# Late queries for heads 8 to 15 in the cross-attention, and the context columns of the first latent batch placed behind the small experts

## The chip, the cores and the metric

The kernel runs on 1 core of one Trainium2 chip, as one program. The metric is the device time of one execution in microseconds (us): 3016.62 us is the median of 3 runs of the kernel before (3016.44 to 3020.77).

A core has five engines that run side by side and meet only at semaphores: TensorE (PE, matmuls; its weight loads are shown as PEld), VectorE (DVE), ScalarE (ACT), GpSimd (POOL) and SyncE (SP, which here only issues transfers). Matmul results land in PSUM, where this kernel holds eight banks: `psG` (four), `psT` (two, for transposes) and `psO` (two, for attention outputs).

## The reference, cut to what matters

Sixteen batches of 112 tokens of width 256 go through four residual blocks. `T` is 112, `D` is 256, `H` is 16 heads of 64, and the context of a batch has `S` = 375 rows.

```
# block 1: self-attention, cross-attention over the context, gated MLP
h1 = adaln(x, t, ...);  x = mha(h1, h1, ...) + x
h2 = adaln(x, t, ...);  x = mha(h2, context, attn2_wq, attn2_wk, attn2_wv, ...) + x
h3 = adaln(x, t, ...);  x = glu_ff(h3, ...) + x

# block 2: 64 small experts (256 -> 128 -> 256), top 8 of them per token, and a shared expert
routed = einsum(expert_act * router_mask, expert_down);  x = x + shared + routed

# block 3: latent attention; keys and values come from the context and the latents together
x = layer_norm(ctx) * ln1_w + ln1_b
lat = layer_norm(layernorm(x_tokens)) * (ln2...) * (1 + scale) + shift
q = lat @ Wq.T;  kv = concat(x, lat) @ Wkv.T            # 375 + 112 = 487 rows
out = softmax(q k / 8) v @ Wo.T

# block 4: 8 large experts, one per token
```

All of it is in f32. The experts' outputs of block 2 are needed by a token before its latent row can be normalised, but the 375 context rows of block 3 depend on the inputs alone.

## The kernel before, in words

**Order of work.** Each engine has its own hand-written instruction stream, in the order of the Python code. A wait is `wait_ge(semaphore, value)`. The class `Tally` counts events, so that both sides of a semaphore know the number they want. Nothing is scheduled by a planner: the order written is the order run.

**Banks for projections.** `bank_for_act` and `bank_for_dve` hand out `psG` banks 0 and 1 to results that ScalarE evacuates, and 2 and 3 to results that VectorE evacuates. Before a bank is reused, PE waits until the evacuation two jobs back is done. `evacuated()` waits for all of them. `held(a, d)` waits for all but the last `a` and `d`, and says which banks the attention must still wait for.

**Block 1** is `batch(b, begin, last)` on each engine, b = 0 to 15. In its cross-attention half PE projects the values of the context (`values2`), transposes the normalised rows `hn2` (`transpose_h`), transposes those of the next batch (`hn1`), projects the queries for heads 0 to 7 (evacuated by ScalarE) and heads 8 to 15 (evacuated by VectorE), runs two small matmuls for the router of the batch before (`tile_ranks`, which wait for a mask that VectorE makes in `choose`), and enters `attention`. There a step `s` of the loop issues the scores of the two heads of pair `s`, the transposes of the probabilities of pair `s-1`, and the value products of pair `s-2`. VectorE takes each head's maximum (`nmax`), ScalarE the exponentials (`probs`); half of the transposes are copied by VectorE, the other half by ScalarE. In the gaps VectorE runs `slots(b-1, i)`, small steps of the router.

**Between block 1 and 2** the last tile is normalised by GpSimd (`normalise_tile`), routed, and its slots are scattered to a table in DRAM (`scatter_tile`). From that the block tables come (`tables0`), then the shared expert (`shared`), in whose loop VectorE also measures the context rows of the first latent batch (`measure_context(0)`), and then GpSimd normalises them (`context_rows(0)`) before it starts the gathers for the experts.

**Block 2** is `blocks0`: 176 blocks of 128 gathered rows. The gathered rows `xg`, their transposes `xT` and the outputs `ysb` lie in the tile that later holds the keys (`flat` is a view of `kT2`). ScalarE stores each output block to `expert_rows` in DRAM.

**Block 3** starts when the stores have landed: GpSimd fetches eight rows for each token (`fetch0`), VectorE adds them up with their weights (`add_rows`, eight instructions) and takes mean and variance (`measure_latents`), GpSimd normalises twice (`latents`, which signals `lat_ready`), PE transposes context and latents together (`transpose_kv`), the copies to `ctxT` apply weight and bias (`copy_kv`), and then come keys (`keysL`, eight products of 487 columns), values (`valuesL`, four chunks of keys, in two halves each) and queries (`queriesL`). `transpose_kv(1)` for the second batch stands before the first attention. From there a steady loop, `batchL`, has each attention followed by the keys and values of the next batch, while VectorE adds the rows of the batch after that.

## Time and profile before

| what | value |
|---|---|
| median of 3 runs | 3016.62 us |
| the profiled execution | 3016.74 us, its span 3015.0 us |
| PE busy | 2805.8 us (93%) |
| DVE busy | 1519.9 us (50%) |
| ACT busy | 1047.2 us (35%) |
| POOL busy | 905.7 us (30%) |
| granted TensorE clock, mean | 0.975 of full speed |
| block 1 | from the start to about 1372 us |
| tables and shared expert | about 1372 to 1437 us |
| block 2, small experts | about 1437 to 1739 us |
| block 3, latent attention | about 1739 to 2798 us |
| tables and block 4, large experts | about 2798 us to the end |

The span is what the profiler saw, from the first to the last instruction of the core. The execution's own time is 1.7 us longer. PE is the engine to look at: where it is busy without gaps at full clock, only fewer matmuls help, and where it stands still, the row behind the gap says who released it. A releaser called "issue" is one that the profile doesn't show. In a timeline row the columns are start, duration, engine, line, operation, output<-input, shapes, count of merged instructions, and in brackets the idle time just before and who ended it. Every f32 matmul appears as two records, so that a projection of 8 matmuls reads x16 (times two chunks of the inner dimension, x16 for four output tiles).

### The profile page before, as it was taken

Reading aid. Unit: us, or ns where it says so; the run is one execution under the profiler, and the core shown is the slowest. Engines: PE = TensorE matmul, PEld = TensorE weight load, DVE = VectorE, ACT = ScalarE, POOL = GpSimd, SP = SyncE. Lnnn points to the kernel's source line nnn. Section 1 sums busy time; section 2 is a strip of 40 time slices with the busy share of each in tenths; the row PEclk is TensorE's granted clock in tenths of the full one; section 3 lists DMA queues with packets and bytes.
Section 4 is the critical chain, followed back from the end, with each engine's and each line's share of the span. In section 5 each row is a group of like instructions: output and inputs, shape, how many; then the busy total and the mean of one; then the engine's idle time right before and its main releaser. Section 6 shows DMA issues by size and latency. Waiting matters only on the chain.

```text
span 3015.0 us, 58447 instructions
## 1 busy us (share of the span) xinstructions
PE 2805.8 (93%) x17275; PEld 1929.8 (64%) x17276; DVE 1519.9 (50%) x4444; ACT 1047.2 (35%) x2721; POOL 905.7 (30%) x1782
## 2 busy tenths in 40 slices
PE   7999999999999999986999948999999999999795
PEld 5777767667777777664788725555555656565574
DVE  4455555555455555555555524555555555554332
ACT  1433333433334333331343313443334433343121
POOL 1021222211221112213555435443443434420212
PEclk9999999999999999997999979999999999999898
DMA  6000000000000000003788831000010000100432
GB/s 218 8 6 7 7 7 7 7 7 7 7 2 7 5 7 7 7 3 118 222 257 266 144 113 33 23 19 19 19 36 20 19 19 26 30 2 3 151 131 61
DMA packets 89264, 154.75 MB, mean 51 GB/s; under 512 B 16964, under 2 KB 64720, under 8 KB 87664
## 3 DMA queue, kind: packets, MB, share of 16 engines
q1 hardware_dynamic: 39760, 85.60, 8.6%
q0 software_dynamic: 21072, 42.53, 6.1%
q10 hardware_dynamic: 28368, 25.83, 2.5%
q8 instruction: 32, 0.52, 0.1%
q14 instruction: 32, 0.26, 0.0%
HBM read 121.93 MB, written 31.98 MB: 51 GB/s over the span
## 4 chain that ended last, share of the span: by engine, by line
PE 85%; DVE 5%; issue 5%; DMA 2%; POOL 1%; ACT 1%; DVEq 0%; POOLq 0%; ACTq 0%
PE psG L895 13%; PE psG L889 13%; PE psG L883 12%; PE psG L905 8%; PE psT L856 7%; PE psO L869 7%; PE psG L841 6%; PE psG L1221 5%; PE psG L1298 2%; PE psO L1313 2%; PE psO L1233 2%; PE psG L1212 1%; DVE nmax L1792 1%; PE psG L805 1%; PE psT L796 1%
## 5 line engine op out<-in xcount | busy, mean ns | idle before, releaser
L895 PE MATMUL psG<-W,ctxT 128*125 128x512 f32 (+2 forms) x896 | 406.7, 597 | 0.0
L1441 ACT ACTIVATE probs<-psG,nmax 112x375 f32<-112x375 f32 (+1 forms) x512 | 317.2, 621 | 237.8 <-DVE nmax L1792 237.8
L889 PE MATMUL psG<-ctxT,W 128*128 128x375 f32 (+1 forms) x1024 | 392.7, 531 | 1.1 <-ACT ctxT L1628 1.1
L1792 DVE TENSOR_REDUCE nmax<-psG 112x1 f32<-112x375 f32 (+1 forms) x512 | 285.2, 601 | 128.6 <-PE psG L841 128.3
L856 PEld LDWEIGHTS psT<-ident,probs 112*125 112x125 f32 (+2 forms) x1792 | 203.2, 166 | 190.6 <-ACT probs L1441 146.8
L883 PE MATMUL psG<-hT,W 128*128 128x112 f32 x2560 | 308.8, 280 | 3.2 <-ACT hT L1466 3.2
L883 PEld LDWEIGHTS psG<-hT,W 128*128 128x128 f32 x2560 | 297.1, 195 | 17.5 <-ACT hT L1466 10.5
L889 PEld LDWEIGHTS psG<-ctxT,W 128*128 128x128 f32 x1024 | 190.1, 190 | 166.5 <-issue 115.1
L856 PE MATMUL psT<-ident,probs 112*125 112x112 f32 (+2 forms) x1792 | 255.6, 278 | 31.9 <-ACT probs L1441 23.6
L895 PEld LDWEIGHTS psG<-W,ctxT 128*125 128x125 f32 (+2 forms) x896 | 159.2, 186 | 173.0 <-issue 171.2
L841 PE MATMUL psG<-kT,qT 64*112 64x375 f32 (+1 forms) x1024 | 249.9, 565 | 11.3 <-ACT ctxT L1628 10.7
L869 PE MATMUL psO<-probsT,v 125*64 125x112 f32 (+2 forms) x3584 | 228.5, 266 | 0.0
L635 POOL DMA_INDIRECT kT<-normed_rows,ids x176 | 166.4, 945 | 138.1 <-PE psG L1212 135.5
L869 PEld LDWEIGHTS psO<-probsT,v 125*64 125x64 f32 (+2 forms) x3584 | 173.5, 136 | 28.6
L1221 PE MATMUL psG<-W,kT 128*128 x704 | 185.9, 386 | 0.2 <-issue 0.2
L905 PE MATMUL psG<-W,oT 128*112 128x256 f32 x768 | 174.7, 381 | 4.0 <-DVE oT L1756 3.9
L1796 DVE COPY probsT<-psT 125x336 f32<-125x336 f32 (+1 forms) x256 | 142.6, 557 | 52.0 <-PE psT L856 52.0
L905 PEld LDWEIGHTS psG<-W,oT 128*112 128x112 f32 x768 | 133.3, 177 | 40.8 <-issue 14.7
L267 POOL TENSOR_SCALAR ve<-mv 112x1 f32<-112x1 f32 x64 | 12.3, 192 | 461.8 <-DVE mv L1844 387.2
L1449 ACT ACTIVATE probsT<-psT 125x336 f32<-125x336 f32 (+1 forms) x256 | 125.4, 490 | 44.0 <-PE psT L856 43.1
L582 POOL DMA_INDIRECT slot_table<-stt,st x128 | 122.4, 957 | 53.1 <-issue 40.2
L659 POOL DMA_INDIRECT mlp<-expert_rows,st x128 | 121.2, 946 | 47.2 <-issue 34.1
(348 smaller groups left out, 4109.5 us busy)
## 6 DMA issues: line engine op xcount, KB each, us to landing
expert_rows<-kT ACTq DMA_DIRECT2D x197, 128.0 KB, 1.8
W<-in_ew SPq DMA_DIRECT2D x64, 384.0 KB, 4.6
W<-in_ew SPq DMA_DIRECT2D x8, 2048.0 KB, 8.8
ctxT<-in_ctxT SPq DMA_DIRECT2D x16, 375.0 KB, 3.1
kT<-in_ctx SPq DMA_DIRECT2D x16, 375.0 KB
W<-in_eb SPq DMA_DIRECT2D x8, 640.0 KB, 10.1
normed_rows<-hrow SPq DMA_DIRECT2D x32, 112.0 KB, 1.9
kT<-normed_rows,ids POOLq DMA_INDIRECT x197, 4.1
```

Of the source, the lines that this page charges most:

```text
L635: nc.gpsimd.indirect_dma_start(out=xg[:, j % 4, :], out_offset=None, in_=hd, in_offset=bass.IndirectOffsetOnAxis(ap=ids[:, j:j + 1], axis= ...
L841: nc.tensor.matmul(psG[0:T, bank, 0:keys], qT[DH * i:DH * i + DH, s, :], kT[DH * i:DH * i + DH, s, 0:keys], start=True, stop=True).then_in ...
L856: mm = nc.tensor.transpose(psT[0:kn, i, c * T:(c + 1) * T], probs[:, 2 * (u % 2) + i, k0:k0 + kn], ident[0:T, 0:T])
L869: mm = nc.tensor.matmul(psO[DH * i:DH * i + DH, u // 4, (u % 4) * T:(u % 4 + 1) * T], v[0:kn, c, h * DH:(h + 1) * DH], probsT[0:kn, u % 2, ...
L883: mm = nc.tensor.matmul(bank[:, j * T:(j + 1) * T], wt[:, c, n0 + j * P:n0 + (j + 1) * P], hT[:, c, :], start=(c == 0), stop=(c == DC - 1))
L889: mm = nc.tensor.matmul(bank[:, 0:n], wt[:, c, n0 + j * P:n0 + (j + 1) * P], src[:, c, 0:n], start=(c == 0), stop=(c == DC - 1))
L895: mm = nc.tensor.matmul(bank[0:kn, 0:512], src[:, c, k0:k0 + kn], wt[:, c, n0 + half * 512:n0 + (half + 1) * 512], start=(c == 0), stop=(c ...
L905: mm = nc.tensor.matmul(bank[0:T, 0:D], oT_[:, c, :], wo[:, c, :], start=(c == 0), stop=(c == n - 1))
L1221: mm = nc.tensor.matmul(psG[:, 2 + j.m2, 0:256], xT[:, j.m2, c, :], weights(c, rank), start=(c == 0), stop=(c == DC - 1))
L1441: nc.scalar.activation(probs[:, 2 * (s % 2) + i, 0:keys], psG[0:T, score_banks(s)[i], 0:keys], ACT.Exp, bias=nmax[:, h:h + 1], accum_out=r ...
L1792: nc.vector.tensor_reduce(nmax[:, 2 * s + i:2 * s + i + 1], psG[0:T, score_banks(s)[i], 0:keys], AXX, ALU.max, negate=True).then_inc(max_r ...
L1796: nc.vector.tensor_copy(probsT[0:size, (s - 1) % 2, 0, 0:nb * T], psT[0:size, 0, 0:nb * T]).then_inc(copied_dve, 1)
```

## The change

It has two parts.

**Late queries (block 1).** The projection for heads 0 to 7 moves ahead of the transposes of `hn1`. The projection for heads 8 to 15 leaves its place ahead of the attention and is issued inside it, in step 1, behind the scores of pair 1 and ahead of the first transposes of probabilities. It goes to bank `psO[:, 1]`, which the attention's value products don't touch before pair 4. VectorE's copy of it moves from ahead of the attention to behind the maxima of pair 1. PE waits for that copy at pair 4.

**Context columns first (block 3).** The transfer of the context rows moves from behind the projection weights to the end of block 1, ahead of the shared expert's weights. VectorE measures them at once, and GpSimd normalises them between `normalise_tile(15)` and `scatter_tile(15)`. The buffers of the experts (`xg0`, `xT0`, `ysb0`) move out of the keys' tile into the weight tile `W`. Behind the experts PE transposes the context alone, makes the keys of its 375 columns and the values of the first three chunks, and only then takes the latents: their transposes, the queries, the latents' 112 key columns (a product of their own) and the last chunk of values. The normalisation of latent batch 0 moves from GpSimd to VectorE (`latents0`). `transpose_kv(1)` moves behind the first attention.

```
 # PE, block 1
+            def late_queries():
+                dve.next()
+                project_T(wq2, hT2, 512, 4, psO[:, 1, :]).then_inc(dve_full, 1)
+                return dve.now()
...
                 values2(2, sides=(1,))
+                pe.wait_ge(w_in["q2"], 16)
+                pe.wait_ge(act_evac, hT2_done)
+                project_T(wq2, hT2, 0, 4, bank_for_act()).then_inc(act_full, 1)
+                q2_done = act.now()
                 if not last:
                     pe.wait_ge(hn1_ready, b + 2)
                     transpose_h(hn1)
-                pe.wait_ge(w_in["q2"], 16)
-                pe.wait_ge(act_evac, hT2_done)
-                project_T(wq2, hT2, 0, 4, bank_for_act()).then_inc(act_full, 1)
-                project_T(wq2, hT2, 512, 4, bank_for_dve()).then_inc(dve_full, 1)
                 if not begin:
                     tile_ranks(b - 1)
-                banks = held(0, 1)
+                pe.wait_ge(act_evac, q2_done)
+                banks = held(1, 1) if not last else held(0, 1)
 # PE, attention: step s of the loop
+                    if s == PAIRS // 2 and late:
+                        pe.wait_ge(dve_evac, queries_done)
...
+                    if s == 1 and late:
+                        queries_done = late()
 # DVE, attention
+                    if s == 1 and late:
+                        late()
                     if s:
                         dve.wait_ge(probsT_ready, u0 + 2 * s - 1)
...
-                copy4(qT2[:, 4:8, :], QSCALE)
 # SP
             sp.wait_ge(dve_evac, BLOCK1_JOBS)
+            sp.dma_start(ctxr[:], a["ctx"][0].rearrange("(c p) d -> p c d", p=SC)).then_inc(ctxr_in, 16)
             sp.dma_start(shw, a["shw"]).then_inc(sh_in, 16)
...
-            sp.dma_start(ctxr[:], a["ctx"][0].rearrange("(c p) d -> p c d", p=SC)).then_inc(ctxr_in, 16)
 # POOL
             normalise_tile(B - 1)
+            context_rows(0, S0.normed)
             scatter_tile(B - 1)
...
-            context_rows(0)
             experts(L0E, S0)
...
-                latents(b)
+                if not isinstance(b, int) or b:
+                    latents(b)
                 fetch0(b + 1, True)
 # buffers of the experts
+        xg0 = W[:, 15104:16128].rearrange("p (u d) -> p u d", u=4)
+        xT0 = W[:, 16128:16640].rearrange("p (u c t) -> p u c t", u=2, c=DC)
+        ysb0 = W[:, 21504:22528].rearrange("p (u d) -> p u d", u=4)
 # PE, block 3
             pe.wait_ge(wL_in, 48)
-            transpose_kv(0)
+            transpose_context(0)
             evacuated()
-            keysL()
-            valuesL(0)
-            rest_L()
-            transpose_kv(1)
+            for j in range(0, IC, 2):
+                keys_T(wkvL, 0, j, ctxT, S, bank_for_act()).then_inc(act_full, 1)
+                keys_T(wkvL, 0, j + 1, ctxT, S, bank_for_dve()).then_inc(dve_full, 1)
+            for c in range(NK - 1):
+                valuesL(c)
+            transpose_latents(0)
+            evacuated()
+            queriesL()
+            project_T(wkvL, ctxT[:, :, S:KV], 0, 4, bank_for_act()).then_inc(act_full, 1)
+            project_T(wkvL, ctxT[:, :, S:KV], 512, 4, bank_for_dve()).then_inc(dve_full, 1)
+            valuesL(NK - 1)
...
                 attention(qT2, kT2, v2, KV, KC, spreadL, banks)
                 dve.skip()
+                if not routed:
+                    transpose_kv(1)
+                    evacuated()
 # DVE, block 3
-            for k in range(L0E.K):
+            copy_context()
+            keysL(None, S)
+            for k in range(4):
+                add_rows(0, k)
+            valuesL(0)
+            for k in range(4, L0E.K):
                 add_rows(0, k)
             measure_latents(0)
-            copy_kv(0)
-            keysL()
+            latents0()
+            valuesL(1)
+            valuesL(2)
+            copy_latents(0)
+            copy4(qT2[:, 4:8, :], QSCALE)
+            copy4(kT2[:, 4:8, S:KV])
+            valuesL(NK - 1)
             for k in range(L0E.K):
                 add_rows(1, k)
             measure_latents(1)
             measure_context(1)
-            valuesL(0)
-            rest_L()
-            copy_kv(1)
```

The order of the instructions, at three places. The first is PE in one of the looped batches of block 1, from the end of the value projections (before) and from the first query projection (after) to the attention. L883 of before and L894 of after are query projections, L911 and L922 the transposes of the next batch's rows, L985 and L996 the router's first matmul, L841 and L850 the scores, L867 the transposes of probabilities. Before:

```order
L895 MATMUL psG<-W,ctxT 125x512 x2
L1029 REGISTER_ALU
L758 REGISTER_ALU
L911 MATMUL psG<-ident,norms 128x112 x2
L1032 REGISTER_ALU
L883 MATMUL psG<-hT,W 128x112 x16
L985 MATMUL psT<-cumr,ones 112x64
L986 MATMUL psT<-mskr,before 112x64
L774 REGISTER_ALU
L841 MATMUL psG<-kT,qT 112x375 x3
L840 REGISTER_ALU
L841 MATMUL psG<-kT,qT 112x375
```

And after:

```order
L894 MATMUL psG<-hT,W 128x112 x8
L1050 REGISTER_ALU
L922 MATMUL psG<-ident,norms 128x112 x2
L996 MATMUL psT<-cumr,ones 112x64
L997 MATMUL psT<-mskr,before 112x64
L1054 REGISTER_ALU
L850 MATMUL psG<-kT,qT 112x375 x2
L849 REGISTER_ALU
L850 MATMUL psG<-kT,qT 112x375 x2
L894 MATMUL psO<-hT,W 128x112 x8
L865 REGISTER_ALU
L867 MATMUL psT<-ident,probs 125x112 x3
```

Eight of the sixteen query matmuls have moved behind the first four scores, and the router's two matmuls now stand behind eight of them instead of sixteen.

The second place is PE between block 2 and the first latent attention. L1327 and L1385 transpose context rows (`v` is the tile they lie in), L1329 and L1394 latents (`R`), L889 and L900 are keys, L895 and L906 values, L883 and L894 queries and, in the kernel after, latent keys. Before:

```order
L1233 MATMUL psO<-W,mlp 128x256
L1327 MATMUL psG<-ident,v 128x125 x3
L1329 MATMUL psG<-ident,R 128x112
L1327 MATMUL psG<-ident,v 128x125 x3
L1329 MATMUL psG<-ident,R 128x112
L889 MATMUL psG<-ctxT,W 128x487 x16
L895 MATMUL psG<-W,ctxT 122x512 x8
L883 MATMUL psG<-ctxT,W 128x112 x16
L895 MATMUL psG<-W,ctxT 122x512 x4
L895 MATMUL psG<-W,ctxT 121x512 x4
L1327 MATMUL psG<-ident,v 128x125 x3
L1329 MATMUL psG<-ident,R 128x112
```

And after:

```order
L1252 MATMUL psO<-W,mlp 128x256
L1385 MATMUL psG<-ident,v 128x125 x6
L900 MATMUL psG<-ctxT,W 128x375 x16
L906 MATMUL psG<-W,ctxT 122x512 x12
L1394 MATMUL psG<-ident,R 128x112 x2
L894 MATMUL psG<-ctxT,W 128x112 x32
L906 MATMUL psG<-W,ctxT 121x512 x4
L850 MATMUL psG<-kT,qT 112x487 x4
```

Keys and three chunks of values now stand ahead of the first instruction that needs a latent, and nothing of the second batch stands ahead of the scores.

The third place is VectorE over the same stretch. L2237 and L2308 add fetched rows, L2261/L2262 and L2331/L2332 measure latents, L2047/L2050 and L1973/L1976 the second context, L2290 and L2367 copy context columns, L2298 and L2389 keys, L2305 and L2396 values, L1856 takes the maxima. Before:

```order
L2315 MEMSET hn 112x8
L2237 SCALAR_TENSOR_TENSOR X<-mlp,wgt,X 112x256 x8
L2261 BN_STATS cst<-X 112x6
L2262 BN_AGGR cmv<-cst 112x2
L2290 TENSOR_SCALAR ctxT<-psG,cols 128x375
L2292 TENSOR_SCALAR ctxT<-psG,affL 128x112
L2298 COPY kT<-psG 128x487 x4
L2237 SCALAR_TENSOR_TENSOR X<-mlp,wgt,X 112x256 x8
L2261 BN_STATS cst<-X 112x6
L2262 BN_AGGR cmv<-cst 112x2
L2047 BN_STATS cst<-kT 125x6 x3
L2050 BN_AGGR cmv<-cst 125x2 x3
```

After, the end of the same stretch, from the last step of `latents0` to the first maxima of the attention:

```order
L2383 TENSOR_SCALAR R<-X,cmv,ry 112x256
L2396 COPY v<-psG 122x512 x2
L2372 TENSOR_SCALAR ctxT<-psG,affL 128x112
L1883 TENSOR_SCALAR qT<-psG 128x448
L1885 COPY kT<-psG 128x4x112
L2396 COPY v<-psG 121x512
L2308 SCALAR_TENSOR_TENSOR X<-mlp,wgt,X 112x256 x8
L2331 BN_STATS cst<-X 112x6
L2332 BN_AGGR cmv<-cst 112x2
L1973 BN_STATS cst<-kT 125x6 x3
L1976 BN_AGGR cmv<-cst 125x2 x3
L1856 TENSOR_REDUCE nmax<-psG 112x1 x4
```

The adding of the second batch's rows has moved from behind the keys to behind the last values, straight ahead of the first attention's maxima.

## Rows read from the trace of the kernel before

**Rows 1.** Waits of PE from 0 to 1345 us: waiter, releaser, total us, times, longest.

```profile
PE psT L856 <- ACT probs L1441: 11.1, 16, 0.8
```

**Rows 2.** Timeline of PE, one batch of block 1, values to pair 5.

```profile
1152.70 1.89 PE L895 MATMUL psG<-W,ctxT 128*125 128x512 f32 x4
...
1154.62 3.74 PE L883 MATMUL psG<-hT,W 128*128 128x112 f32 x32
...
1158.64 1.52 PE L841 MATMUL psG<-kT,qT 64*112 64x375 f32 x8
1160.86 1.13 PE L856 MATMUL psT<-ident,probs 112*125 112x112 f32 x6 [0.70 <-ACT probs L1441]
...
1163.12 1.06 PE L856 MATMUL psT<-ident,probs 112*125 112x112 f32 x6 [0.31 <-ACT probsT L1449]
...
1164.83 0.89 PE L841 MATMUL psG<-kT,qT 64*112 64x375 f32 x4
...
1169.59 0.89 PE L841 MATMUL psG<-kT,qT 64*112 64x375 f32 x4
```

**Rows 3.** Timeline of DVE in the same batch.

```profile
1154.63 0.69 DVE L1821 COPY v<-psG 125x512 f32<-125x512 f32 x1 [2.15 <-PE psG L895]
...
1157.01 0.19 DVE L1865 TENSOR_SCALAR mskr<-repr 112x64 f32<-112x64 f32 x1
1158.39 0.62 DVE L1811 TENSOR_SCALAR qT<-psG 128x448 f32<-128x448 f32 x1 [1.20 <-PE psG L883]
```

**Rows 4.** Timeline of ACT in the same batch: the copy of the first queries.

```profile
1156.68 0.54 ACT L1460 ACTIVATE qT<-psG 128x448 f32<-128x448 f32 x1 [0.89 <-PE psG L883]
```

**Rows 5.** Timeline of PE between the small experts and the second latent batch's keys.

```profile
1776.61 0.86 PE L1327 MATMUL psG<-ident,v 125*128 125x125 f32 x3 [37.81 <-issue]
...
1822.56 0.89 PE L1327 MATMUL psG<-ident,v 125*128 125x125 f32 x3 [9.43 <-POOL R L691]
...
1829.02 1.37 PE L856 MATMUL psT<-ident,probs 112*122 112x112 f32 x8
...
1851.61 13.36 PE L889 MATMUL psG<-ctxT,W 128*128 128x487 f32 x32
```

**Rows 6.** Timeline of DVE: adding rows of batches 0 and 1, and what follows.

```profile
1760.43 4.61 DVE L2237 SCALAR_TENSOR_TENSOR X<-mlp,wgt,X 112x256 f32<-112x256 f32 x8 [22.50 <-DMA mlp<-expert_rows,st]
...
1796.44 4.60 DVE L2237 SCALAR_TENSOR_TENSOR X<-mlp,wgt,X 112x256 f32<-112x256 f32 x8
...
1803.15 1.25 DVE L2305 COPY v<-psG 122x512 f32<-122x512 f32 x2
```

**Rows 7.** Timeline of DVE: one inverse root in block 1, first and last.

```profile
1148.30 0.18 DVE L1697 BATCH_NORM_AGGREGATE mv<-st 112x2 f32<-112x6 f32 x1
...
1151.36 0.41 DVE L1699 TENSOR_SCALAR hn<-R,mv,ry 112x256 f32<-112x256 f32 x1
```

**Rows 8.** Timeline of POOL: last slots, context rows, end of the first latents.

```profile
1390.01 0.19 POOL L578 COPY st<-sloti 112x8 int32<-112x8 int32 x1 [11.47 <-DVE sloti L1883]
...
1414.31 0.26 POOL L256 TENSOR_SCALAR cve<-cmv 128x3 f32<-128x3 f32 x1
...
1419.27 3.65 POOL L676 TENSOR_SCALAR v<-kT,cmv,cry 125x256 f32<-125x256 f32 x3 [0.18 <-POOL cry L262]
...
1775.90 0.61 POOL L691 TENSOR_TENSOR R<-R,ry 112x256 f32<-112x256 f32 x1
```

**Rows 9.** Timeline of DVE beside those context rows.

```profile
1421.51 0.28 DVE L2037 SCALAR_TENSOR_TENSOR repr<-iotaf,tofr,mskr 112x64 f32<-112x64 f32 x1
...
1421.90 0.43 DVE L2037 SCALAR_TENSOR_TENSOR repr<-iotaf,tofr,mskr 112x64 f32<-112x64 f32 x1
```

**Rows 10.** Timeline of PE at the end of block 1: projections behind a gap.

```profile
1354.96 0.41 PE L911 MATMUL psG<-ident,hn 112*128 112x112 f32 x2 [4.94 <-DVE hn L1699]
1356.30 10.20 PE L883 MATMUL psG<-hT,W 128*128 128x112 f32 x64 [0.93 <-ACT hT L1466]
```

**Rows 11.** Busy time by stretch: us, PE, PEld, DVE, ACT, POOL, PEclk, DMA share, GB/s.

```profile
1740.00:1760.00 20.00, 0.00 (x0) 0.00 (x0) 0.00 (x0) 0.00 (x0) 7.64 (x9) 0.53 0.84 320
```

More of the change, by code:

```diff
@@ L562, in _, with context_rows @@
             norm1(0)
+            def context_rows(b, done=None):
+                wait_apart(pool, ctx_stats, b + 1)
+                inverse_root(nc.gpsimd, chain, cry[:, 0:NS], cmv[:, 0:NS, 1], crt[:, 0:NS], cve[:, 0:NS])
+                for c in range(NS):
+                    e = nc.gpsimd.tensor_scalar(ctxn[:, c, :], ctxr[:, c, :], cmv[0:SC, c, 0:1], cry[0:SC, c:c + 1],
+                                            ALU.subtract, ALU.mult)
+                    if done and c == NS - 1:
+                        e.then_inc(done, 1)
             def normalise_tile(r):
@@ L829, in self_outputs, with attention @@
                 mm.then_inc(outputs_ready, 1)
-            def attention(qT, kT, v, keys, size, spread, banks={}, fill=None):
+            def attention(qT, kT, v, keys, size, spread, banks={}, fill=None, late=None):
                 ch = chunks(keys, size)
@@ L1782, in self_copy, with attention @@
                 nc.vector.tensor_copy(probsT[0:T, u // 2, u % 2, :], psT[0:T, u % 2, 0:4 * T]).then_inc(copied_dve, 1)
-            def attention(keys, size, spread, between=None):
+            def attention(keys, size, spread, between=None, late=None):
                 nb = len(chunks(keys, size))
@@ L1982, in _ @@
                 measure_tile(B - 1, i)
+            chain(nc.vector.memset(cmv[:], 0.0))
+            measure_context(0)
             def blocks_of_experts(s, E):
@@ L2253, in _ @@
             tables0()
-            chain(nc.vector.memset(cmv[:], 0.0))
             shared()
```

128 lines of the change are left out of this document (88 added, 40 removed).

## The prediction

> **What bounds the kernel now.** I read the busy time by stretch first, then PE's waits, then the timelines of PE, VectorE, ScalarE and GpSimd at the two places that the change touches. PE is busy 93% of the span, so nearly all of the time is matmuls at full clock, and the change removes none. What it can win is idle time of PE. Two kinds bear on it.
>
> In block 1 each of the 16 batches has one wait for the first probabilities of the cross-attention, 11.1 us in all [rows 1]. In the batch shown it is 0.70 us, and 0.31 us follow at the second pair [rows 2]. The first pair has nothing behind it that PE could do: scores, maximum, exponential, and only then a transpose. (PE's clock there is full; the pairs from pair 3 on come every 2.38 us, (1169.59 - 1164.83)/2, without a wait.)
>
> Between blocks 2 and 3 PE stands still for 37.81 us, from 1738.80 to 1776.61, and again for 9.43 us ahead of 1822.56 [rows 5]. The first gap is a chain: stores of the last expert rows land, GpSimd fetches rows, VectorE adds from 1760.43 to 1765.04 [rows 6], statistics and GpSimd's two inverse roots until 1776.51 [rows 8]. The second is the same chain for the second batch. In the first the granted clock falls to 0.53 [rows 11], which is the 1.2 GHz level, and what follows runs slowly.
>
> **Late queries, step by step.** Before, values end and the next row starts at 1154.43 (1152.70 + 1.89, less 0.16 by which records overlap). From there to the scores of pair 3 at 1164.83 it is 10.40 us [rows 2]. After, on the same clock of the batch:
>
> - Eight query matmuls: half of 3.74 less the overlap of 0.17, 1.79, to 1156.22. The transposes of the next rows, 1154.62 - 1154.43 = 0.19, to 1156.41.
> - The router's matmuls need the mask, which VectorE ends at 1157.20. It starts from the last value copy at 1154.63, which waits for PE [rows 3], so it doesn't come earlier. PE, which used to arrive at 1158.19, now waits 0.8 us (0.84 with 0.05 for the semaphore, an estimate). This is a new stall, and it takes most of what the change gives. The router itself takes 1158.64 - 1158.19 = 0.45, to 1157.70.
> - The copy of the first queries: ScalarE started it 2.06 us behind the projection's start and took 0.54 [rows 4], so now about 1157.03. That is hidden by the wait for the mask. In batch 0, with no router, it is the stall itself, 0.7 us against the 0.45 us of work that batch doesn't have, and the gain comes out alike.
> - Scores of two pairs, 1.52, to 1159.22. Late queries, 1.79, to 1161.0. Maxima and exponentials of pair 0 start with the scores, 0.94 us earlier than before, and are ready at about 1159.9: the 0.70 us wait is gone.
> - First transposes, about 0.85, then scores, transposes and products at the steady 2.38, to 1164.2.
>
> The gain is 1164.83 - 1164.2 = 0.6 to 0.7 us. I take 0.7 for each of the 16 batches: 11 us. VectorE's copy of 0.62 us [rows 3] moves into the attention, between the maxima of pair 1 and the copy of the first transposes. By my count that copy then ends near 1162.4, and PE wants it at 1162.7; the cover is 0.3 us, and if it is gone, up to the 0.62 us is lost. Bounds for a batch: from 0.1 us (0.7 less 0.62) to 1.4 us (both waits and the 0.4 us of slower records behind them gone, and no wait for the mask). The wait at pair 4 for the copy has over 5 us of cover.
>
> **Moves at the end of block 1.** GpSimd's context rows take 1422.92 - 1414.31 = 8.6 us, and now stand ahead of the last scatter. GpSimd is idle 11.47 us there before the slots come at 1390.01 [rows 8], so they cost nothing, with nearly 3 us of cover. The transfer for them must land within some 6 us of the end of block 1; its landing isn't shown, and what it costs past the cover I bound at 6 us. On VectorE 1.4 us of measuring leave the shared expert's loop, but the loop then waits that much longer for the table rows' transfer. I take 0, from 0 to 1.4 us gained.
>
> A VectorE operation of the router that reads two tensors took 0.28 us beside those context rows, and once 0.43 us [rows 9]. The Trainium skill, page "SBUF — State Buffer", section "SBUF: two separate sides", says that VectorE and GpSimd share one pair of ports, and that an operation of VectorE with two SBUF inputs and one of GpSimd shut each other out for a whole instruction. By that rule each of the three row operations of GpSimd could hold the router's chain. The row shows 0.15 us where it would be 1.2 (3.65 / 3). I go by the row, and keep the rule as a rival below.
>
> **Behind the small experts.** Before, from the last expert matmul at 1738.80 to the second batch's keys at 1851.61: 112.8 us [rows 5]. After:
>
> - Context transposes and their copies, as now about 1 us each: keys start at 1740.7. Keys of 375 columns: 13.36 at full clock [rows 5] x 375/487 = 10.3, to 1751.0. There the clock is still full. Five half-chunks of values at 1.73 (1.89 less overlap) [rows 2]: to 1759.7.
> - The sixth half needs VectorE's copy of the first, which is queued behind four added rows. These start when the fetched rows land, 1760.43 [rows 6], as before, since stores and fetch don't change. Four take 2.3, the copy 0.69: PE goes on at 1763.4, to 1765.1.
> - VectorE adds the other four to 1765.7 and measures to 1766.3. The two inverse roots take 1151.36 - 1148.48 = 2.9 each on VectorE [rows 7], and with the scaling it is 6.6 in all: latents at 1772.9. On GpSimd, from the last added row at 1765.04 to 1776.51, it was 11.5 with the 0.7 of statistics [rows 6, 8]. PE waits 7.8 us.
> - Transposes, two value copies queued ahead on VectorE, the copies of the latents: PE starts at 1774.5. Queries and latent keys are 32 records of 112 columns each, 3.6 as in [rows 2], and the last values 3.5: 10.7. Behind a gap the clock is low: 64 such records took 10.20 us behind 4.94 us of idle [rows 10] where twice 3.7 is 7.4. That costs 2.8. To 1788.0.
> - Now the first attention. VectorE must copy the last values (0.7) and then runs what used to be hidden under the keys and values: from 1796.44 to 1803.15 it is 6.7 us [rows 6]. The maxima start at 1795.5, the first transposes at 1796.9. PE has its scores done at 1790.2 and waits 6.7 us.
> - From there to the attention's end it is 22.6 us (1829.02 to 1851.61 [rows 5]), and 2.8 more for the clock: 1822.3. GpSimd's context rows and latents of batch 1 start at 1795.5 and take 8.6 and 10.8: ready at 1814.9, so the 9.43 us gap is gone. Transposes and copies, 2.4, stand open: keys at 1824.7.
>
> The gain is 1851.61 - 1824.7 = 27 us. Behind it the loop is unchanged: the rows of batch 2 land at about 1828, when they are wanted. Bounds: 33 us if the two slow restarts cost nothing, 20 us if another 7 us chain (as the one just described) opens at the second batch.
>
> The sum against the execution of 3016.74: 3016.7 - 11 - 27 = 2978.7. The median is 0.1 us lower than that execution, so I predict 2979 us.
>
> **Rivals.** A: the router's mask costs nothing, because VectorE's chain comes earlier once the attention ahead is shorter. Against it: the mask starts from PE's own values. 16 x 1.4 = 22 us, so 2968. Chance 0.10.
>
> B: VectorE becomes the bound of each cross-attention. Between the maxima it has two router steps and a copy, some 2.3 us a pair by its timeline (an estimate), against PE's 2.38, and 0.62 comes on top at pair 1. For it: it is that near. Against it: the router steps end at pair 5, and PE doesn't wait for VectorE in those pairs now. The late queries then give 0.1 us a batch, 1.6 in all: 2988. Chance 0.17.
>
> C: the context columns don't do what is said: PE's work goes forward but each piece waits on VectorE's order, and a further chain of 7 us opens like the one that batch 1's rows open above (the second context, whose load waits for the first latents, or the second fetch). 20 us: 2986. Chance 0.13.
>
> D, by the page's rule: each of the three row operations holds the router's chain 1.2 us, 3.6 in all: 2982. Chance 0.04.
>
> E, slower: the experts' gathered rows now lie in the tile where the expert weights land, and each of the 176 blocks gets slower by it. The stage takes about 302 us (1437 to 1739), 1.72 a block. A fifth more, which is an assumption, is 0.34 x 176 = 60, and 2979 + 60 = 3039. It decides from 38/176 = 0.22 us a block on. Nothing in the rows speaks for it. Chance 0.02.
>
> **How the numbers follow.** The forecast has the other 0.54, with its own range of 2973 to 2984. The range for 8 in 10 reaches over B and C up to 2991, and down to A's 2968. 0.2% is 6 us, about what tells a change from none here. All cases but E are 25 us or more below 3016.6; I give 0.96 to faster, 0.02 to within 0.2% and 0.02 to slower.
>
> **What would show it.** In the profile after: the wait for probabilities at the first pair gone, one of 0.8 us for the mask ahead of the router's matmul in 15 batches, and the batch 0.7 us shorter; keys at full clock right behind the experts; three gaps of PE of about 3.5, 7.8 and 6.7 us in place of 37.81 and 9.43; second keys at about 113 - 27 = 86 us behind the last expert matmul. A gap of PE for VectorE's copies in pairs 1 to 4 speaks for B, blocks of 2 us in block 2 for E. The forecast is wrong if the stage from the experts to the second keys is longer than 93 us, or a batch of block 1 less than 0.3 us shorter.

## The result and the profile after

The changed kernel takes 2981.29 us (median of 4 runs, 2980.08 to 2982.93), the kernel before beside it 3017.82. The ratio is 0.9878, with an interval of 0.9861 to 0.9895. The forecast was 2979.0 with a range of 2968 to 2991. A second comparison later gave 2985.59 us and 0.989 (0.9875 to 0.9905), so that two medians of the same kernel lie 4.3 us apart.

The profiled spans are 3015.0 and 2979.9 us, 35.1 apart. I cut both at five places: the first and last write of a batch's result in block 1 (VectorE), the first transposes and the last weight load of the small experts (PE), and the start of the second latent batch's keys.

| stretch, us | before | after | difference |
| --- | --- | --- | --- |
| start to first write | 132.4 | 131.8 | -0.6 |
| 15 batches of block 1, write to write | 1239.0 | 1230.1 | -8.9 |
| last write to first expert transposes | 65.9 | 65.2 | -0.7 |
| small experts | 300.9 | 304.0 | +3.1 |
| experts to second keys | 113.4 | 85.5 | -27.9 |
| second keys to the end | 1163.4 | 1163.4 | 0 |

The first and the fourth row vary from one profile to the next: over all the runs below the start took 130.1 to 132.8 us (132.8 in the changed kernel's second profile), and the small experts 300.9 to 304.1.

PE's waits from 0 to 1345 us (waiter, releaser, total us, times, longest):

```profile
PE psT L996 <- DVE mskr L1937: 10.6, 15, 0.8
...
PE psG L850 <- ACT qT L1507: 0.5, 1, 0.5
PE psT L867 <- ACT probsT L1496: 0.2, 1, 0.2
```

The wait for the first probabilities [rows 1] is gone, and the one for the mask has come in 15 batches. In batch 0, which has no router, it is the copy of the first queries, 0.5 us. The timeline of PE in one batch, which answers to [rows 2] (start, duration, engine, line, output<-input, shapes, count, idle before):

```profile
1147.13 1.93 PE L894 MATMUL psG<-hT,W 128*128 128x112 f32 x16
...
1149.96 0.41 PE L996 MATMUL psT<-cumr,ones 112*112 112x64 f32 x2 [0.70 <-DVE mskr L1937]
...
1151.94 2.04 PE L894 MATMUL psO<-hT,W 128*128 128x112 f32 x16
1153.82 0.82 PE L867 MATMUL psT<-ident,probs 112*125 112x112 f32 x6
...
1155.42 0.90 PE L867 MATMUL psT<-ident,probs 112*125 112x112 f32 x6
...
1156.98 0.89 PE L850 MATMUL psG<-kT,qT 64*112 64x375 f32 x4
```

From the queries' start to the scores of pair 3 it is 9.85 us, where [rows 2] give 10.40 from 1154.43. VectorE in the same batch, the end of its maxima of pair 1, the late copy, and the copy of the first transposes:

```profile
1153.26 0.99 DVE L1856 TENSOR_REDUCE nmax<-psG 112x1 f32<-112x375 f32 x2
1154.17 0.61 DVE L1876 TENSOR_SCALAR qT<-psO 128x448 f32<-128x448 f32 x1
1154.70 0.49 DVE L1862 COPY probsT<-psT 125x336 f32<-125x336 f32 x1
```

It has no idle time between them. Behind the small experts, PE's rows that answer to [rows 5]:

```profile
1730.43 1.29 PE L1252 MATMUL psO<-W,mlp 128*128 x4
...
1733.60 10.36 PE L900 MATMUL psG<-ctxT,W 128*128 128x375 f32 x32 [1.24 <-ACT ctxT L1681]
...
1756.25 1.98 PE L906 MATMUL psG<-W,ctxT 128*122 128x512 f32 x4 [3.72 <-DVE v L2396]
1765.88 1.04 PE L1394 MATMUL psG<-ident,R 112*128 112x112 f32 x2 [7.65 <-DVE R L2383]
1767.46 9.31 PE L894 MATMUL psG<-ctxT,W 128*128 128x112 f32 x64 [0.54 <-ACT ctxT L1686]
...
1780.14 1.92 PE L850 MATMUL psG<-kT,qT 64*112 64x487 f32 x8
1789.40 1.78 PE L867 MATMUL psT<-ident,probs 112*122 112x112 f32 x8 [7.34 <-ACT probs L1488]
1791.11 1.97 PE L850 MATMUL psG<-kT,qT 64*112 64x487 f32 x4
...
1816.55 3.92 PE L900 MATMUL psG<-ctxT,W 128*128 128x487 f32 x9 [1.11 <-ACT ctxT L1675]
```

In place of gaps of 37.81 and 9.43 us there are three of 3.72, 7.65 and 7.34. VectorE between the second and the third (here with what it adds for batch 1, [rows 6]):

```profile
1773.23 0.62 DVE L1883 TENSOR_SCALAR qT<-psG 128x448 f32<-128x448 f32 x1 [5.87 <-PE psG L894]
1776.80 0.62 DVE L1885 COPY kT<-psG 128x448 f32<-128x448 f32 x1 [2.95 <-PE psG L894]
1780.24 0.69 DVE L2396 COPY v<-psG 121x512 f32<-121x512 f32 x1 [2.82 <-PE psG L906]
1780.85 0.48 DVE L2308 SCALAR_TENSOR_TENSOR X<-mlp,wgt,X 112x256 f32<-112x256 f32 x1
...
1787.92 2.34 DVE L1856 TENSOR_REDUCE nmax<-psG 112x1 f32<-112x487 f32 x4
```

It stands idle 11.6 us in the copies, and then adds rows and measures for 7.1 us while PE waits for its maxima. Busy time of PE by stretch (us, PE busy, granted clock, DMA share, GB/s) shows what the gaps do to the clock:

```profile
1766.00:1772.00 6.00, 5.32 (x25) 0.54 0.52 143
1772.00:1780.00 8.00, 8.00 (x51) 1.00 0.00 0
1780.00:1790.00 10.00, 2.65 (x12) 0.76 0.00 1
1790.00:1797.00 7.00, 7.00 (x40) 0.61 0.00 1
```

At the end of block 1, VectorE and GpSimd (answering to [rows 8, 9]):

```profile
1368.60 1.08 DVE L1973 BATCH_NORM_STATS2 cst<-kT 125x6 f32<-125x256 f32 x3 [5.46 <-DMA kT<-in_ctx]
...
1376.85 0.48 DVE L1948 TENSOR_TENSOR cumr<-cumr,mskr 112x64 f32<-112x64 f32 x1
...
1378.24 0.38 DVE L1951 SCALAR_TENSOR_TENSOR repr<-iotaf,tofr,slotr 112x64 f32<-112x64 f32 x1
```

```profile
1375.48 3.73 POOL L573 TENSOR_SCALAR v<-kT,cmv,cry 125x256 f32<-125x256 f32 x3 [0.18 <-POOL cry L265]
1381.02 0.19 POOL L592 COPY st<-sloti 112x8 int32<-112x8 int32 x1 [1.81 <-DVE sloti L1955]
```

### The profile page after: what moved, and what is told of

It is laid out like the page before. It is cut to its first block and busy times, and to the rows that moved or that the text cites. A ratio compares the mean times of both kernels' runs of the same rounds, so it can differ in the third digit from the quotient of the medians.

```text
span 2979.9 us, 58472 instructions
## 1 busy us (share of the span) xinstructions
PE 2801.7 (94%) x17307; PEld 1931.6 (65%) x17308; DVE 1524.5 (51%) x4468; ACT 1029.3 (35%) x2709; POOL 899.5 (30%) x1757
## 5 line engine op out<-in xcount | busy, mean ns | idle before, releaser
L906 PE MATMUL psG<-W,ctxT 128*125 128x512 f32 (+2 forms) x896 | 406.9, 597 | 3.7 <-DVE v L2396 3.7
L900 PE MATMUL psG<-ctxT,W 128*128 128x375 f32 (+1 forms) x1024 | 386.8, 525 | 2.3 <-ACT ctxT L1681 1.2
L1856 DVE TENSOR_REDUCE nmax<-psG 112x1 f32<-112x375 f32 (+1 forms) x512 | 284.9, 601 | 130.5 <-PE psG L850 130.2
L867 PEld LDWEIGHTS psT<-ident,probs 112*125 112x125 f32 (+2 forms) x1792 | 202.1, 167 | 168.1 <-ACT probs L1488 110.7
L900 PEld LDWEIGHTS psG<-ctxT,W 128*128 128x128 f32 x1024 | 189.0, 189 | 163.1 <-issue 106.7
L894 PEld LDWEIGHTS psG<-hT,W 128*128 128x128 f32 x2304 | 268.7, 194 | 24.9 <-ACT hT L1513 16.2
L894 PE MATMUL psG<-hT,W 128*128 128x112 f32 x2304 | 279.1, 280 | 3.2 <-ACT hT L1513 3.2
L906 PEld LDWEIGHTS psG<-W,ctxT 128*125 128x125 f32 (+2 forms) x896 | 159.2, 186 | 176.8 <-issue 170.2
L867 PE MATMUL psT<-ident,probs 112*125 112x112 f32 (+2 forms) x1792 | 249.5, 277 | 23.3 <-ACT probs L1488 19.6
L850 PE MATMUL psG<-kT,qT 64*112 64x375 f32 (+1 forms) x1024 | 248.3, 563 | 11.4 <-ACT ctxT L1675 10.3
L650 POOL DMA_INDIRECT W<-normed_rows,ids x176 | 166.3, 945 | 150.0 <-PE psG L1231 142.9
L1240 PE MATMUL psG<-W 128*128 x704 | 186.0, 387 | 0.2 <-issue 0.2
L916 PEld LDWEIGHTS psG<-W,oT 128*112 128x112 f32 x768 | 133.3, 177 | 40.8 <-issue 14.7
L674 POOL DMA_INDIRECT mlp<-expert_rows,st x128 | 121.4, 948 | 47.2 <-issue 34.1
```

The costliest lines, as they stand in the source:

```text
L650: nc.gpsimd.indirect_dma_start(out=xg0[:, j % 4, :], out_offset=None, in_=hd, in_offset=bass.IndirectOffsetOnAxis(ap=ids[:, j:j + 1], axis ...
L850: nc.tensor.matmul(psG[0:T, bank, 0:keys], qT[DH * i:DH * i + DH, s, :], kT[DH * i:DH * i + DH, s, 0:keys], start=True, stop=True).then_in ...
L867: mm = nc.tensor.transpose(psT[0:kn, i, c * T:(c + 1) * T], probs[:, 2 * (u % 2) + i, k0:k0 + kn], ident[0:T, 0:T])
L894: mm = nc.tensor.matmul(bank[:, j * T:(j + 1) * T], wt[:, c, n0 + j * P:n0 + (j + 1) * P], hT[:, c, :], start=(c == 0), stop=(c == DC - 1))
L900: mm = nc.tensor.matmul(bank[:, 0:n], wt[:, c, n0 + j * P:n0 + (j + 1) * P], src[:, c, 0:n], start=(c == 0), stop=(c == DC - 1))
L906: mm = nc.tensor.matmul(bank[0:kn, 0:512], src[:, c, k0:k0 + kn], wt[:, c, n0 + half * 512:n0 + (half + 1) * 512], start=(c == 0), stop=(c ...
```

## The experiments

The theory: late queries win 0.6 us a batch, because the mask costs what the probabilities used to; the move behind the experts wins 28 us and is bounded by VectorE's order; some 3 us are lost in the experts' stage for a reason to be found, if they aren't a spread between runs. Rivals: the experts' buffers in the weights' tile cost those 3 us (E); VectorE bounds the attention (B).

### Each part alone

The first edit is the late queries alone, on the kernel before (all hunks on `attention(..., late)`, `late_queries` and the order in `batch`); the second is everything but them.

> The kernel before with the late queries alone (with the copies reordered as the change has them); nothing at the end of block 1 or behind the small experts is changed. Theory (the two parts add up; in the profile of the changed kernel the late queries give 9.5 us by the end of block 1): 3017.8 - 9.5 = 3008 us, and the 37.8 us gap ahead of the first queries behind block 2 stays. Rival (each of the 16 batches gains what my walk said, 0.7 us, and the context rows' moves took some back): 3006.5. Rival B (VectorE bounds the attention): 3016.

> The kernel before with all of the change but the late queries: context load and rows at the end of block 1, first batch's context columns behind the small experts, experts' buffers in the weights' tile. Theory (parts add up): -0.5 at the end of block 1, +1.2 ahead of the experts, -3.1 in the experts' stage, +28.0 behind them, a gain of 25.6 us: 2992 us. If the 3.1 us that the experts' stage got longer is not due to this part but varies from run to run, the stage is 301.5 us here and the time 2989.

In this comparison every kernel took some 115 us longer than in the others (the kernel before 3132.83 us; the last section comes back to it). The two took 3121.72 and 3111.15, with ratios of 0.9963 (0.9949 to 0.9976) and 0.9932 (0.9918 to 0.9945). The first fits its theory, the second gained less than either of its two values (2992 of 3017.8 is 0.9914). Both were compared once more, beside the kernel before at 3015.65.

> The kernel before with the late queries alone, once more, since its first comparison fell where every kernel took 115 us longer. In the profile of the changed kernel the mask costs 0.70 us in 15 batches and the first probabilities nothing. Theory: block 1 ends 9.5 us earlier, time 9 to 12 us under the kernel before. The experts' stage, here with its buffers where they were, tells on the 3 us by which it was longer in the changed kernel: 301 us if the buffers' place did that, 303 to 304 if the earlier end of block 1 or the landing of the gathered rows did.

> The kernel before with all of the change but the late queries, once more, for the same reason. Theory: 28 us gained behind the experts, up to 3 lost in their stage and about 0.5 at the end of block 1: 24 us under the kernel before. With the late queries' 9.5 it must make the 33.4 us that the changed kernel gave in the last comparison.

Late queries alone: 3006.26 us, ratio 0.9972 (0.9961 to 0.9983), 9.4 us. The rest alone: 2987.44, ratio 0.9907 (0.9891 to 0.9922), 28.2 us. The first is what was expected (9 to 12 us), the second 4 us more than expected, mostly because the 3 us that were put down as lost in the experts' stage weren't lost here (301.3 us). The product of the ratios is 0.9879, and the changed kernel has 0.9878 and 0.989. By the cuts of the table above, the first has 1229.9 us for the 15 batches and 112.2 behind the experts, the second 1238.8 and 85.4. The changed kernel has 1230.1 and 85.5. So in both stages the parts add up, and neither shares a gain with the other; the times alone, with intervals of 3 to 5 us on either side, wouldn't show it as sharply.

### The experts' buffers

```
-    out=xg[:, j % 4, :], out_offset=None, in_=hd,
+    out=xg0[:, j % 4, :], out_offset=None, in_=hd,
...
-    nc.scalar.activation(ysb[:, j.m, :], psO[:, j.m2, 0:D], ACT.Copy)
+    nc.scalar.activation(ysb0[:, j.m, :], psO[:, j.m2, 0:D], ACT.Copy)
```

> The kernel before with one edit: the small experts' gathered rows, their transposes and their outputs lie in the weights' tile, as in the changed kernel. Theory 1 (the place costs time: 3.1 us over 176 blocks, 18 ns a block): 3021 us, experts' stage 304.6 us from its first transposes to its last matmul. Theory 2 (the place costs nothing; the 3.1 us come from a transfer or a scheduling that the other moves changed, or vary from run to run): 3017.8 us, stage 301.5.

It took 3133.04 us against 3132.83, ratio 1.0003 (0.9994 to 1.0012). The weight loads of the experts' last product, by line (min, median and max ns, first and last start):

```profile
L1236 PEld LDWEIGHTS psO<-W,mlp x352: 186/191/193, 1550.5 to 1847.2; 128*128 128x128 f32 x176
```

In the kernel before these loads take 186/190/192. The stage takes 301.5 us from its first transposes (1545.7). The place costs nothing that can be seen, and rival E is out: over all the kernels here the stage took 301.3 to 304.1 us with the buffers moved (the 301.3 is the context part alone), and 300.9, 301.2 and 303.0 with the buffers where they were.

What makes it 301 or 304 stays open. Each part alone had 301.2 and 301.3, but 303.0 and 302.9 in the comparison where all took longer; both together had 304.0 and 303.4, but 301.9 with the doubled copy further below, which touches block 1 alone. The same kernel thus differs by up to 1.8 us from one comparison to another, and the kernel before was profiled once (300.9), so it isn't shown that the change costs anything here. One piece can be named, PE's waits for gathered rows, before and after:

```profile
PE psG L1212 <- DMA kT<-normed_rows,ids: 0.3, 1, 0.3
```

```profile
PE psG L1231 <- DMA W<-normed_rows,ids: 2.1, 5, 1.0
```

That is 1.8 of the 3.1 us, and 1.0 of the 2.5 in the second profile (1.3 us of waits). But the parts alone have 0.8 and 1.4 us of such waits in stages of 301.2 and 301.3, so it isn't all of it.

### Filling the wait for the mask

```
+    project_T(wq2, hT2, 512, 2, psO[:, 1, :])
     if not begin:
         tile_ranks(b - 1)
...
-    project_T(wq2, hT2, 512, 4, psO[:, 1, :]).then_inc(dve_full, 1)
+    project_T(wq2, hT2, 768, 2, psO[:, 1, 2 * T:4 * T]).then_inc(dve_full, 1)
```

> The changed kernel, with two of the four late query chunks (eight matmuls, about 0.9 us) issued ahead of the router's ranks instead of behind the scores of pair 1, where TensorE waits 0.70 us a batch for the router's mask. Theory (that wait is PE's own idle time and can be filled, and the first probabilities are ready by the time the other half is through): the wait for the mask falls from 10.6 us to under 1, no new wait above 0.2 us a batch, gain 0.7 x 15 = 10 us: 2971 us. Rival (the mask's wait only moves: with 0.9 us less work behind the scores of pair 1 the wait for probabilities comes back): up to 0.7 us a batch waits there again, and the time stays at 2981.

3099.93 us, ratio 0.9899 (0.9884 to 0.9914), beside the 3132.8 us. The two parts alone make 0.9963 x 0.9932 = 0.9895 there, so no gain can be told. Of PE's waits from 100 to 1450 us this one is new (the list also has 35.4 us for "issue" and 9.8 us for ScalarE's copies of probabilities, which the late queries alone have in about the same stretch of the same comparison, 37.5 and 9.7):

```profile
PE psT L867 <- ACT probs L1489: 10.7, 14, 0.8
```

The mask's wait is gone from the list, and the rival's wait has come, as large (0.76 us in a batch). But who makes it? VectorE in one batch:

```profile
967.63 1.00 DVE L1857 TENSOR_REDUCE nmax<-psG 112x1 f32<-112x375 f32 x2 [0.52 <-PE psG L850]
968.55 0.21 DVE L1949 TENSOR_TENSOR cumr<-cumr,mskr 112x64 f32<-112x64 f32 x1
...
969.47 1.00 DVE L1857 TENSOR_REDUCE nmax<-psG 112x1 f32<-112x375 f32 x2
```

The scores of both pairs were there at 968.2 (966.71 and 1.52 us in PE's timeline), and their maxima start at 969.47, behind router steps of the batch before. ScalarE is named in the wait, but these rows say that VectorE's order makes it late. So the next run moves those steps one pair later:

```
-    attention(S, SC, spreadA, ... lambda s: slots(b - 1, s), late_queries)
+    attention(S, SC, spreadA, ... lambda s: slots(b - 1, s - 2), late_queries)
```

> The changed kernel with half of the late queries ahead of the router's ranks, as in the run before (where the 0.70 us wait for the mask went and one of 0.76 us for the probabilities of pair 1 came in its place: 10.7 us, 14 times), and VectorE's router steps inside the attention one pair later, so that the maxima of pair 1 start 0.9 us earlier. Theory (those router steps, not ScalarE or the late copy, made that wait): both waits are under 0.2 us a batch, gain 0.7 x 15 = 10 us against the changed kernel. Rival (the wait is ScalarE's two exponentials and TensorE's own order): the 0.76 us stays, gain 0.

2973.13 us against 2985.59 for the changed kernel in the same comparison; the 15 batches take 1219.3 us instead of 1230.5, which is 0.75 a batch. PE's waits from 100 to 1345 us have neither of the two (a last one, 0.2 us, stands once):

```profile
PE psG L922 <- DVE hn L1764: 4.9, 1, 4.9
PE psG L916 <- DVE oT L1821: 3.6, 16, 0.3
...
PE psT L867 <- ACT probsT L1497: 0.2, 1, 0.2
```

The theory holds, with 12.5 us between the medians where 10 were expected: the wait for the mask was PE's own idle time, and could be filled once VectorE's order allowed it. In the rows of a batch the four maxima of pairs 0 and 1 now stand together, 1.91 us from 1141.53, with no router step between them. The later router steps weren't run without the split queries.

### The cover of the late copy

```
+    chain(nc.vector.tensor_scalar(qT2[:, 4:8, :], psO[:, 1, 0:4 * T]..., QSCALE, None, ALU.mult))
     nc.vector.tensor_scalar(qT2[:, 4:8, :], psO[:, 1, 0:4 * T]..., QSCALE, None, ALU.mult)
```

> The changed kernel with VectorE's copy of the late queries done twice (0.6 us and a hand-over of 0.1 more in every batch of block 1). The prediction gave that copy 0.3 us of cover behind the maxima of pair 1. Theory (cover 0.3 us, the rest opens a wait for VectorE's copy of the first probabilities): 0.3 to 0.4 us a batch, 5 to 6 us slower than the changed kernel. Rival (VectorE bounds the attention already, so the copy is paid in full): 0.7 x 16 = 11 us. Rival (over 0.7 us of cover): 0.

It took 2992.85 us, ratio 0.9924 (0.9911 to 0.9938): 0.0034 to 0.0046 above the changed kernel's two ratios, 10 to 14 us. The 15 batches take 1242.0 us, 0.78 more each than in the changed kernel. PE's waits from 100 to 1345 us:

```profile
PE psT L867 <- DVE probsT L1862: 10.4, 15, 0.7
```

The second copy adds 0.72 us to VectorE (start to start), and 0.70 of it shows in PE. The first rival is right: the cover is 0.02 us at most, not 0.3. The rows of one batch tell why, VectorE's and PE's:

```profile
1163.19 0.61 DVE L1876 TENSOR_SCALAR qT<-psO 128x448 f32<-128x448 f32 x1
1163.91 0.62 DVE L1878 TENSOR_SCALAR qT<-psO 128x448 f32<-128x448 f32 x1
1164.45 0.50 DVE L1862 COPY probsT<-psT 125x336 f32<-125x336 f32 x1
```

```profile
1165.17 0.90 PE L867 MATMUL psT<-ident,probs 112*125 112x112 f32 x6 [0.70 <-DVE probsT L1862]
```

From the copy's recorded end (1164.95) to PE's start it is 0.22 us. In the changed kernel the copy ends at 1155.19, and PE goes on at 1155.42, without a wait but also 0.23 us later: what looks like cover between the rows is the hand-over.

### VectorE's order behind the experts

```
     copy_latents(0)
+    measure_context(1)
     copy4(qT2[:, 4:8, :], QSCALE)
+    for k in range(4): add_rows(1, k)
     copy4(kT2[:, 4:8, S:KV])
-    valuesL(NK - 1)
-    for k in range(L0E.K): add_rows(1, k)
+    for k in range(4, L0E.K): add_rows(1, k)
     measure_latents(1)
-    measure_context(1)
+    valuesL(NK - 1)
```

> The changed kernel once more, beside the three below. In the last comparison the kernel before took 3132.8 us instead of 3017.8, with TensorE waiting for no work item ahead of the first self-attention queries of each batch of block 1 (25.7 us in ten batches). The late queries alone gave 11.7 us there (ratio 0.9963) and the rest alone 21.7 (0.9932). Theory (the parts add up): 33 to 36 us under the kernel before, wherever that stands. Rival (the two parts share a gain, or cost each other one): under 30 or over 40.

> The changed kernel with VectorE's queue between the first latents and the first attention behind block 2 in another order: the second context is measured and the second batch's eight rows are added in the gaps in which VectorE waits for the queries, the latent keys and the last values (5.87, 2.95 and 2.82 us), not behind them. Theory (the 7.34 us wait of TensorE for the first probabilities is VectorE's 7 us of added rows and measuring, and the rows have landed by 1771): the wait falls to about 1 us, gain 6.3 us, and 0 to 2 more if TensorE's clock comes back sooner. Rival (the fetched rows land later than that, so that VectorE waits for them ahead of the copy of the latent keys, and TensorE with it): gain under 3 us, a wait for a DMA in VectorE's queue.

The changed kernel again: 2985.59 us against 3018.99, 33.4 apart, the theory's lower end. With the rows earlier: 2976.22, ratio 0.9857 (0.9842 to 0.9872), 9.4 us less. From the experts to the second keys it is 76.7 us instead of 85.4. PE:

```profile
1785.80 1.26 PE L867 MATMUL psT<-ident,probs 112*122 112x112 f32 x8 [0.65 <-ACT probs L1488]
1786.98 1.07 PE L850 MATMUL psG<-kT,qT 64*112 64x487 f32 x4
```

The wait is 0.65 us, 6.7 less, and the other 2 us are the clock's: the second scores take 1.07 us here, behind that short gap, and 1.97 in the changed kernel, behind 7.34 us. From the first transposes to the second keys it is 24.6 us instead of 27.2, while from the latents' transposes to the first scores it is 14.7 instead of 14.3. The gain is a little above the 6.3 to 8.3 us of the theory. The rows had landed, but the second context had not. The rival's wait for a DMA is there, for another transfer, and cost nothing, since PE waits for no copy behind it:

```profile
1774.70 1.08 DVE L1973 BATCH_NORM_STATS2 cst<-kT 125x6 f32<-125x256 f32 x3 [4.76 <-DMA kT<-in_ctx]
```

### The latents' chain on GpSimd

```
     def batchL(b, turned, routed):
-        if not isinstance(b, int) or b:
-            latents(b)
+        latents(b)
...
-    latents0()
```

> The changed kernel with the first latents normalised by GpSimd, as before, not by VectorE. The prediction priced VectorE's chain at 6.6 us (7.5 in the trace with the statistics) against 11.5 on GpSimd. Theory: TensorE's wait for the latents grows from 7.65 to about 11.7 us, GpSimd's second fetch starts later but still lands before it is wanted, 4 us slower than the changed kernel. Rival (GpSimd's queue decides: the second fetch, now behind the latents, holds the second batch's rows, and so VectorE ahead of the first attention): 8 us slower or more.

2984.34 us, ratio 0.9898 (0.9883 to 0.9913), 2 to 6 us above the changed kernel by the two ratios, with intervals that overlap. The trace is sharper: 88.6 us from the experts to the second keys instead of 85.5, and

```profile
1768.14 0.64 PE L1393 MATMUL psG<-ident,R 112*128 112x112 f32 x2 [10.52 <-POOL R L698]
...
1792.02 1.78 PE L866 MATMUL psT<-ident,probs 112*122 112x112 f32 x8 [6.98 <-ACT probs L1487]
```

The chain from the last added row to the latents is 11.5 us there (1756.6 to 1768.1) and 7.5 in the changed kernel (1758.4 to 1765.8). Of the 4.0 us, 3.1 reach the keys. VectorE waits for no row of the second fetch there, so its rival is out.

### All three edits together

The split queries, the later router steps, the rows earlier, and two value copies of VectorE ahead of the added rows.

> The changed kernel with the edits of the two runs above, and VectorE's first two value copies of the first latent batch ahead of its added rows (TensorE waits 3.72 us for the first of them). Expected: 6.3 us behind block 2 and 10 us in block 1 as above, and 0.7 to 1.4 us because the copies no longer stand between the rows and the latents: 17 to 18 us under the changed kernel, 1.7% under the kernel before.

2963.41 us (2959.39 to 2964.89), ratio to the kernel before 0.9816 (0.9803 to 0.983), 22.2 us under the changed kernel. The two edits alone gave 12.5 and 9.4, more than the 10 and 6.3 that the 17 to 18 us were added up from. The value copies, expected to give 0.7 to 1.4, gave nothing I can see (76.5 us against 76.7): the 3.7 us gap joins the next one, which is 11.40:

```profile
1752.07 0.64 PE L1395 MATMUL psG<-ident,R 112*128 112x112 f32 x2 [11.40 <-DVE R L2386]
```

This is the fastest version of the study.

## Why the prediction was right

**Late queries: right in kind, 11 us forecast, 9.5 measured** (8.9 in 15 batches; the 0.6 of the start is within what it varies by, and the late queries alone gave 9.4). The walk through the batch holds step by step. The mask's wait is 0.70 us (0.8 forecast), the router's first matmul comes 2.83 us behind the queries' start (2.82), the late queries 4.81 (4.79), the first transposes 6.69 (6.57), the scores of pair 3 9.85 (9.77). The late queries' records take 0.1 us more than half of the old ones, and I rounded the walk's 0.63 up to 0.7. Measured 0.59.

**The cover of 0.3 us for VectorE's late copy: wrong.** It is nothing, as the doubled copy shows. The walk had the copy of the first transposes end 7.97 us behind the queries' start and PE ready for it at 8.27; the trace has 8.06 and 8.29. What failed is that I took all between them for cover and left out the hand-over of 0.2 us. It cost the forecast nothing, because the copy just fits, but of 0.72 us more on VectorE 0.70 were paid in every batch. Rival B is out as a forecast (no wait for VectorE in these pairs), but its mechanism was one step away, and it appeared as soon as the mask's wait was filled.

**Moves at the end of block 1: 0 forecast.** VectorE's cast of the last slots comes 18.82 us behind the last write (1361.89 to 1380.71); GpSimd still waits 1.81 us for it, so the context rows are hidden, with less cover than the 3 us that I gave. From the last write to the experts it was 64.4 to 69.6 us in the runs, 65.9 before and 65.2 after, so that no loss can be told apart. VectorE waited 5.46 us for the context's transfer, which landed 6.25 us behind its issue (1362.35 to 1368.60), so just not within the 6 us that I had asked for: the copy of the router's transposes (1370.02) now starts straight behind the measuring, 0.2 us later behind the last write than before, and the transfer has no cover left. The slots come 0.5 us later behind the last write than before (18.29); the two slowed rows of rival D are some 0.36 of that, the late copy most of the rest.

**Rival D.** Beside GpSimd's three row operations, VectorE's addition of two tensors took 0.48 us (0.23 at this place in the kernel before), and one of the steps behind it 0.38 where the others take 0.28 or 0.29: 0.4 us in all, not 3.6. The Trainium skill, page "SBUF — State Buffer", section "SBUF: two separate sides", has the two shut each other out for a whole instruction of the one that started first, and a row operation takes 1.2 us here (3.73 / 3). This trace disagrees: six of VectorE's operations with two SBUF inputs start between 1376.85 and 1379.13, while GpSimd's rows run (1375.48 to 1379.21), and none takes more than 0.25 us above its usual time. The measurement decides.

**Behind the experts: 27 us forecast, 28.0 measured** (112.8 less 84.8). The milestones behind the last expert matmul's end (1731.7), forecast in brackets: keys at 1.9 (1.9), the sixth half-chunk of values at 24.5 (24.6), latents ready at 34.1 (34.1), queries at 35.7 (35.7), first scores at 48.4 (49.2), first transposes at 57.7 (58.1), second keys at 84.8 (85.9). The term that was a little off is the slow restart: 64 records took 9.31 us instead of 10.20, with the clock at 0.54 from 1766 to 1772 us and at 1.00 behind that. In the attention the slow restart cost 2.4 us where 2.8 were forecast (25.0 us to the attention's end, 25.4 forecast).

**The experts' stage: 0 forecast, 2.5 to 3.1 us longer in the two profiles.** I had no term for it. The runs show that it isn't the buffers' place. Since the same kernel differs there by up to 1.8 us between two comparisons, and variants of the changed kernel had 301.9 to 304.1 us against one profile of the kernel before, a cost of the change itself isn't shown.

**How near the sum came is in part luck.** The profiled execution of the changed kernel took 2981.6 us, the sum said 2978.7. The gain was 1.5 us too high for the late queries, and 1.0 and 0.7 too low behind the experts and ahead of them; these nearly cancel, and the 3.1 us of the experts' stage are left. The whole miss is less than the 4.3 us between two medians of the changed kernel. What the runs bear out is the two large terms, each measured alone.

Rival A is out (the mask costs 10.6 us), and C is out (no further chain; the next context and fetch were in time).

## What to carry to other kernels

When a wait is moved off a pair of engines, walk the waiting engine and the one that releases it to the next hand-over: here the late queries removed one wait of 0.70 us and opened another of 0.70, and only filling it, with VectorE's queue reordered so that no third one opened, brought the second half of the gain. The engine that the profile names as releaser may itself have waited for another engine's order. An engine with idle stretches of 5.87, 2.95 and 2.82 us and then 7 us of work that another waits for wants its work moved into those stretches, which here took moving a few lines; and the gap removed on PE paid twice here (6.7 us of wait, and 2 us because the records behind it ran at full clock).

## What the runs showed of the hardware that I had not expected

One comparison ran where every kernel took 115 us longer (the kernel before 3132.8 us). The record names chip 9 for it, and chips 14 and 8 for the other two with experiments; whether it was the chip or the hour isn't known, since that chip stands for one comparison only. Nearly all of it lies in block 1: 1348.9 us for the 15 batches in the kernel with the buffers alone moved, instead of the 1239.0 of the kernel before. PE's waits from 400 to 1300 us in that kernel:

```profile
PE psG L886 <- issue: 25.7, 45, 1.1
```

The kernel before, profiled in another comparison, has none of these. They fall on the projections in the last pairs of the cross-attention, and behind them the granted clock is at its lower level for some 7 to 10 us in each of the four batches between 900 and 1190 us. One of them:

```profile
1176.00:1182.00 6.00, 5.12 (x22) 0.55 0.01 0
1182.00:1188.00 6.00, 6.00 (x46) 0.59 0.00 0
```

So idle time of some 2.6 us a batch, in four or five pieces, goes with 7.3 us a batch (109.9 / 15). What holds PE's instructions there the profile doesn't show, and it wasn't tried. Behind the experts the context part took 91.1 us there instead of 85.4. The late queries alone came out alike in both comparisons (ratios of 0.9963 and 0.9972), the context part less so (0.9932 and 0.9907, 21.7 and 28.2 us), so that a time of one comparison can't be set beside a time of the other.
